# First block of a four-layer kernel: selection ahead of the angles, tokens in another order, sums and weights split, column product on VectorE

## The reference

```
xn   = layernorm(x);   x2 = layernorm(xn) * g_in + b_in
s    = (xn Wq)(ctx Wk)^T per head (4 heads, 77 keys), masked
keep the 32 largest scores of each row; softmax over them; mean of the heads, token mask
film = (attention @ ctx Wv) @ [W_film_in, W_film_out] + biases, times a gate
xk   = x2 * (1 + film_in_gain) + film_in_shift
K[d, l] = 2 Re sum_n dC[d, n] exp(dtA[d, n] l),  l = 0..511      (S4D kernel)
y    = causal convolution of xk with K (by a transform of length 1024) + xk * D_skip
xt   = y * (1 + film_out_gain) + film_out_shift + xn
x    = x + layernorm(xt + gelu(layernorm(xt) W1 + b1) W2 + b2) * g_out + b_out
```

## Time and profile before

| | us |
|---|---|
| median of 3 runs (lowest, highest) | 630.66 (626.01, 631.53) |
| the profiled execution | 629.79 |
| its span | 628.0 |
| PE busy in the span | 499.5 |
| DVE busy | 376.9 |
| ACT busy | 269.4 |
| POOL busy | 157.4 |

### The profile page before, as it was taken

How to read it: one execution, slowest core, us unless ns; L and a number is a source line. 1 busy time by engine, 2 the same in 40 slices (tenths; PEclk the granted TensorE clock), 3 DMA queues, 4 the chain that set the end, 5 groups by cost and what they waited for, 6 DMA issues and landing times.

```text
span 628.0 us, 9151 instructions
## 1 busy us (share of the span) xinstructions
PE 499.5 (80%) x3063; PEld 354.9 (57%) x3063; DVE 376.9 (60%) x1354; ACT 269.4 (43%) x830; POOL 157.4 (25%) x187
## 2 busy tenths in 40 slices
PE   4383689879893589995767774998999999879977
PEld 2132679868661256774545543675566666548845
DVE  5499973134537556763466744775444444589866
ACT  3688433340131366652243442662222222199643
POOL 5999952003215500001300452110000000110032
PEclk9557766979896699997565677897999999999999
DMA  8200000000318000000000103000000000000001
GB/s 312 110 1 1 3 2 2 0 1 1 134 32 353 1 1 2 1 3 1 1 7 23 32 11 91 0 3 1 1 1 1 1 0 1 1 2 0 2 1 33
DMA packets 9636, 18.36 MB, mean 29 GB/s; under 512 B 947, under 2 KB 8179, under 8 KB 9078
## 3 DMA queue, kind: packets, MB, share of 16 engines
q1 hardware_dynamic: 9590, 17.79, 7.8%
HBM read 16.00 MB, written 1.79 MB: 28 GB/s over the span
## 4 chain that ended last, share of the span: by engine, by line
PE 62%; POOL 15%; DVE 13%; ACT 4%; issue 3%; DMA 1%; ACTq 0%; SPq 0%; DVEq 0%; POOLq 0%
PE bank L1755 6%; PE bank L1756 6%; PE bank L1766 5%; PE bank L726 3%; PE bank L1010 3%; PE bank L757 3%; PE bank L1941 2%; PE bank L1054 2%; POOL rstd L205 2%; PE bank L1033 2%; DVE stats L196 2%; ACT arenaB L1957 2%; POOL arenaA L608 2%; PE bank L1917 2%; PE bank L1629 2%
## 5 line engine op out<-in xcount | busy, mean ns | idle before, releaser
L204 POOL TENSOR_SCALAR rtmp<-mv 128x4 f32<-128x4 f32 x22 | 5.1, 230 | 333.5 <-DVE mv L190 333.5
L1807 DVE TENSOR_TENSOR arenaB<-arenaB,bank 128x512 f32<-128x512 f32 x40 | 27.5, 688 | 54.7 <-PE bank L1756 53.8
L1777 ACT ACTIVATE arenaB<-bank 128x512 f32<-128x512 f32 x40 | 23.9, 597 | 76.7 <-PE bank L1755 76.7
L1766 PEld LDWEIGHTS bank<-arenaA,arenaB 128*128 128x128 f32 x320 | 38.7, 192 | 9.1 <-issue 9.1
L1755 PE MATMUL bank<-xnT,arenaA 128*128 128x512 f32 x80 | 42.7, 617 | 0.0
L1756 PE MATMUL bank<-xnT,arenaA 128*128 128x512 f32 x80 | 41.7, 604 | 0.0
L1766 PE MATMUL bank<-arenaA,arenaB 128*128 128x128 f32 x320 | 38.8, 275 | 0.0
L1957 ACT ACTIVATE arenaB<-bank,arenaB 128x77 f32<-128x77 f32 x88 | 27.1, 349 | 5.1 <-DVE arenaB L1980 5.1
L240 PE MATMUL bank<-in_ctx,xn 128*128 128x128 f32 x56 | 14.5, 382 | 18.5 <-DVE xn L211 18.4
L1065 DVE TENSOR_REDUCE nmax<-bank 128x1 f32<-128x512 f32 x32 | 20.5, 684 | 11.1 <-PE bank L1010 11.1
L1756 PEld LDWEIGHTS bank<-xnT,arenaA 128*128 128x128 f32 x80 | 15.7, 196 | 20.2 <-issue 20.2
(11 more groups left out here) (475 smaller groups left out, 1296.0 us busy)
## 6 DMA issues: line engine op xcount, KB each, us to landing
arenaA<-in_moe_dram SPq DMA_DIRECT2D x1, 3840.0 KB, 12.4
in_dft<-in_dft_dram SPq DMA_DIRECT2D x1, 2048.0 KB, 10.2
in_dft<-in_head_dram SPq DMA_DIRECT2D x1, 2048.0 KB, 7.6
arenaA<-in_l_dram SPq DMA_DIRECT2D x1, 2048.0 KB, 16.9
vw_scratch<-in_dft SPq DMA_DIRECT2D x32, 38.5 KB
arenaB<-vw_scratch SPq DMA_DIRECT2D x2, 576.0 KB, 4.9
in_rows<-in_rows_dram SPq DMA_DIRECT2D x1, 842.5 KB, 7.3
in_ctx<-in_ctx_dram SPq DMA_DIRECT2D x1, 653.0 KB, 4.3
```

Of the source, the lines that this page charges most:

```text
L1766: ins = nc.tensor.matmul(bank[4 + m % 3][:, q4 * P:(q4 + 1) * P], hid2[:, m % 2, c, q4 * P:(q4 + 1) * P], w[:, 2 * HE + c * P:2 * HE + (c ...
L1777: nc.scalar.activation(sil2[:, n % 3, :], bank[n % 2][:], ACT.Silu).then_inc(silu_ready, 1)
L1807: Vv.tensor_tensor(hid2[:, m % 2, c, :], sil2[:, n % 3, :], bank[2 + n % 2][:], ALU.mult).then_inc(hid_ready, 1)
```

## The change

- **Token order.** Tile q, partition 32g + a now holds token 16a + 4g + q, for x, the masks, the transform tables, `altrow` and `alt` (which gets two columns). In this order `pe_kernel`'s output [32 a, (d, b)] can be copied straight to `kx` by four copies, one for each quarter g. `pe_kernel_turn` and its copies are gone, as is the `unfold` matrix. The input is loaded, and the output stored, by four transfers of 32 partitions each.
- **Loads.** x goes ahead of `ctx`; `dft` is loaded after the phases, because the angles `uG` use its place till then.
- **Selection first.** On ScalarE all score copies go ahead of the angles, the decays between them; the sines come after x2, the first exponents, `vfilm` and `fold1`. On VectorE group 0's four rounds go ahead of `vec_s4`.
- **Column product** from GpSimd to VectorE (`vec_s4_columns`), between group 1's first and second round. `pool_rstd_twice` moves ahead of the `uG` angles, `pool_x2` of batch 0 ahead of the gains.
- **Masks and weights.** `vec_keep0` is split in `vec_mask0` and `vec_weight0`; `vec_film(1)` goes ahead of group 3's rounds.
- **TensorE.** film(1) ahead of kernel(2), the first batch's transform around kernel(3). The Nyquist sums of both batches and the kernel are one call after film(3), and their product one VectorE instruction (`vec_nyquist`).
- **ScalarE.** `act_dft` goes behind film(2) and the sums of group 3.
- **Feed-forward** batch by batch: turn 0, first product 0, turn 1, second product 0, first product 1, second product 1. The hidden values move from arenaA to arenaB. The last layer's weight sums move behind the last film group (ScalarE) and behind the feed-forward (TensorE).

The core of the diff (indentation shortened by eight columns):

```diff
--- before.py
+++ after.py
...
 kny = sb("kny", 1, D)
 yny = sb("yny", 1, NB, D)
 xt = sb("xt", P, NT, D)
-hT0 = part(arenaA, 8192, 4, TOK)
+hT0 = part(arenaB, 0, 4, TOK)
 altrow = arenaA[0:1, 11776:11776 + S]
 consts_set, ctx0_mm, ctx0_copy, bias_rows = sem("consts_set"), sem("ctx0_mm"), sem("ctx0_copy"), sem("bias_rows")
...
-vH, uG = part(arenaB, 4928, D, LH), part(arenaB, 2464, D, LB)
-rH, hh4, eH = part(arenaA, 0, D, LH), part(arenaA, 2176, D, LA), part(arenaA, 6272, D, LA)
+vH, uG = part(arenaA, 0, D, LH), part(packed["dft"], 0, D, LB)
+rH, hh4, eH = part(arenaB, 8416, D, LH), part(arenaA, 2176, D, LA), part(arenaA, 6272, D, LA)
 gg4, sG, eG = (part(arenaB, 8416 + 2048 * i, D, LB) for i in range(3))
-ka = part(arenaA, 6272, D, LB)[0:LA]
-kTl = part(arenaA, 3200, S)
+V_H, V_GC, V_GS, V_HH = 3, 4, 5, 6
 s4_vec, s4_pe, s4_inverses = sem("s4_vec"), sem("s4_pe"), sem("s4_inverses")
+def quarters():
+    return [slice(LA * g, LA * (g + 1)) for g in range(P // LA)]
+def tokens(v, g):
...
 def sync_loads(sp):
-    for k in ("cols", "ctx"):
-        sp.dma_start(packed[k][:], A[k]).then_inc(loaded[k][0], 16)
-    sp.dma_start(X[:], A["x"].rearrange("(t p) d -> p t d", p=P)).then_inc(x_loaded, 16)
+    sp.dma_start(packed["cols"][:], A["cols"]).then_inc(loaded["cols"][0], 16)
+    for g, r in enumerate(quarters()):
+        sp.dma_start(X[r].rearrange("p (b q) d -> p b q d", b=NB), tokens(A["x"], g)).then_inc(x_loaded, 16)
+    sp.dma_start(packed["ctx"][:], A["ctx"]).then_inc(loaded["ctx"][0], 16)
     sp.dma_start(packed["s4"][:], A["s4"]).then_inc(loaded["s4"][0], 16)
     sp.dma_start(masks8[:], A["masks"].partition_broadcast(P)).then_inc(masks_loaded, 16)
     sp.dma_start(tmask8[:], A["tmask"]).then_inc(masks_loaded, 16)
...
     sp.dma_start(altrow, A["altrow"]).then_inc(bias_rows, 16)
-    for k in ("dft", "l3f", "l1", "ffn0", "small0", "l2"):
+    for k in ("l3f", "l1", "ffn0", "small0", "l2"):
         sp.dma_start(packed[k][:], A[k]).then_inc(loaded[k][0], 16)
+    sp.wait_ge(s4_vec, V_GS)
+    sp.dma_start(packed["dft"][:], A["dft"]).then_inc(loaded["dft"][0], 16)
     sp.wait_ge(y_mm, 2 * NB)
     sp.dma_start(packed["head0"], A["head0"]).then_inc(loaded["head0"][0], 16)
...
                 ins = nc.vector.match_replace(r0[:, t, h, :], top0[:, t, h, 8 * k:8 * k + 8], src[:, t, h, :], NEVER)
         st.link(ins)
-def vec_keep0(dve, st, g):
+def vec_mask0(dve, g):
     for t in GROUPS[g]:
         dve.wait_ge(e0_ready, t + 1)
         nc.vector.scalar_tensor_tensor(e0[:, t], r0[:, t], 0.5 * NEVER, e0[:, t], ALU.is_lt, ALU.mult).then_inc(em_ready, 1)
+def vec_weight0(dve, st, g):
     r = slice(2 * g, 2 * g + 2)
     dve.wait_ge(sums_ready, 2 * g + 2)
...
-A_ARE, A_ANG, A_VH, A_UG, A_GAIN, A_HH = 2, 3, 4, 5, 6, 7
+A_ARE, A_ANG, A_VH, A_UG, A_GAIN = 2, 3, 4, 5, 6
...
     dve.wait_ge(s4_pool, A_VH)
-    vec_phase(st, rH, vH, V["quarter"]).then_inc(s4_vec, 1)
+    vec_phase(st, vH, rH, vH, V["quarter"]).then_inc(s4_vec, 1)
     dve.wait_ge(s4_pool, A_UG)
-    vec_phase(st, gg4, uG, V["quarter"]).then_inc(s4_vec, 1)
-    ins = vec_phase(st, sG, uG, V["off2"])
+    dve.wait_ge(s4_vec, V_H)
+    vec_phase(st, gg4, gg4, uG, V["quarter"]).then_inc(s4_vec, 1)
+    vec_phase(st, sG, sG, uG, V["off2"]).then_inc(s4_vec, 1)
+    dve.wait_ge(s4_vec, V_GS)
+def vec_s4_columns(dve):
+    dve.wait_ge(s4_act, E_COLS)
+    for d in range(0, D, D // 8):
+        r = slice(d, d + D // 8)
+        ins = nc.vector.tensor_tensor(hh4[:, r], hh4[:, r], eH[:, r], ALU.mult)
     ins.then_inc(s4_vec, 1)
-    dve.wait_ge(s4_vec, 5)
 em1, half_sin, full_sin, u0, inv_a2, u1, u2, u3 = (q[i][:] for i in (0, 1, 2, 3, 4, 5, 6, 7))
...
+    pool_rstd_twice(pool, st, 0, False)
     for r in (slice(i * n, (i + 1) * n) for i in range(4)):
         ins = tt(uG[:, r], bc(ang[:, r], P, n, LB), V["iotab"].unsqueeze(1).broadcast_to([P, n, LB]), ALU.mult)
     ins.then_inc(s4_pool, 1)
-def pool_s4_columns(pool):
-    pool.wait_ge(s4_act, 4)
-    for d in range(0, D, D // 8):
-        r = slice(d, d + D // 8)
-        ins = nc.gpsimd.tensor_tensor(hh4[:, r], hh4[:, r], eH[:, r], ALU.mult)
-    ins.then_inc(s4_pool, 1)
-def pool_s4_rows(pool, st):
+def pool_s4_rows(pool, st, slices):
...
-def act_s4_decay(act):
-    A_ = nc.scalar.activation
+def act_s4_tanh(act):
     act.wait_ge(s4_pool, A_ARE)
-    A_(q[0][:], are[:], ACT.Tanh, scale=0.5).then_inc(s4_act, 1)
-    for m in range(LA):
-        a = LA // 2 - 1 - m if m < LA // 2 else m
-        ins = A_(eH[:, :, m], are[:], ACT.Exp, scale=float(LB * a))
-    ins.then_inc(s4_act, 1)
+    nc.scalar.activation(q[0][:], are[:], ACT.Tanh, scale=0.5).then_inc(s4_act, 1)
+def act_s4_decay(act, part):
+    for a in part:
+        ins = nc.scalar.activation(eH[:, :, a], are[:], ACT.Exp, scale=float(LB * a))
+    if part[-1] == LA - 1:
+        ins.then_inc(s4_act, 1)
...
-    A_(hh4[:, :, LA // 2:LA], rH[:, :, 0:LA // 2], ACT.Sin, scale=-TURN, bias=V["qturn"])
-    A_(hh4[:, :, 0:LA // 2], rH[:, :, 1:LH], ACT.Sin, scale=V["lowturn"], bias=V["qturn"]).then_inc(s4_act, 1)
+def act_s4_columns(act):
+    A_ = nc.scalar.activation
+    act.wait_ge(s4_vec, V_H)
+    A_(hh4[:, :, LA // 2:LA], vH[:, :, 0:LA // 2], ACT.Sin, scale=-TURN, bias=V["qturn"])
+    A_(hh4[:, :, 0:LA // 2], vH[:, :, LA // 2:0:-1], ACT.Sin, scale=V["lowturn"], bias=V["qturn"]).then_inc(s4_act, 1)
...
-    pe.wait_ge(s4_pool, A_HH + 1 + i)
+    pe.wait_ge(s4_vec, V_HH)
+    pe.wait_ge(s4_pool, A_GAIN + 1 + i)
     if i >= 2:
...
                                hh4[:, d, :], gg4[:, d, :], start=True, stop=True)
     ins.then_inc(kern_pe, 1)
-def pe_kernel_turn(pe):
-    pe.wait_ge(kern_act, 4)
-    for b in range(LB):
-        ins = nc.tensor.matmul(bank[2][:, b * LA:(b + 1) * LA], ka[:, :, b], V["unfold"][0:LA], start=True, stop=True)
-    ins.then_inc(kern_pe, 1)
-    pe.wait_ge(kern_act, 5)
-    for j in range(TB):
-        ins = nc.tensor.transpose(bank[3][:, j * P:(j + 1) * P], kTl[:, j * P:(j + 1) * P], ident)
-    ins.then_inc(kern_pe, 1)
...
 def act_kernel(act, i):
     per = 512 // LB
     act.wait_ge(kern_pe, i + 1)
-    nc.scalar.copy(ka[:, i * per:(i + 1) * per, :], bank[2 + i % 2][0:LA, :].rearrange("p (d b) -> p d b", b=LB)).then_inc(kern_act, 1)
...
+    for g, r in enumerate(quarters()):
+        src = bank[2 + i % 2][0:LA, :].rearrange("p (d b) -> p b d", b=LB)[:, g * TB:(g + 1) * TB, :]
+        ins = nc.scalar.copy(kx[r, :, i * per:(i + 1) * per], src)
+    ins.then_inc(kern_act, 1)
...
-def pe_nyquist(pe, parts, b):
-    pe.wait_ge(film_ready, TB * (b + 1))
-    for at, v in enumerate(parts):
+def pe_nyquist(pe):
+    pe.wait_ge(xk_ready, NT)
+    for at, v in enumerate((xk[:, 0], xk[:, 1], kx)):
         for q4 in range(TB):
-            ins = nc.tensor.matmul(bank[7][0:1, at * D:(at + 1) * D], V["alt"], v[:, q4], start=(q4 == 0), stop=(q4 == TB - 1))
+            ins = nc.tensor.matmul(bank[4][0:1, at * D:(at + 1) * D], V["alt"][:, q4 % 2:q4 % 2 + 1], v[:, q4], start=(q4 == 0), stop=(q4 == TB - 1))
     ins.then_inc(dft_mm, 1)
...
         tt(out[:, :, 0], pr[:, 0, :, 0], pr[:, 1, :, 1], ALU.subtract)
         tt(out[:, :, 1], pr[:, 1, :, 0], pr[:, 0, :, 1], ALU.add).then_inc(prod_ready, 1)
         dve.wait_ge(prod_ready, 3 * b + jj + 1)
-    dve.wait_ge(kf_ready, 2 + b)
-    tt(yny[:, b], yny[:, b], kny[:], ALU.mult).then_inc(prod_ready, 1)
+def vec_nyquist(dve):
+    dve.wait_ge(kf_ready, 2)
...
     n = 0
     for b in range(NB):
+        pe_turn(pe, ln_done, NT * 1, tmp2, [b])
+        if b:
+            pe_ffn0_down(pe, 0)
         pe.wait_ge(ln_T, NB * 1 + b + 1)
         for c in range(4):
             if n >= 4:
                 pe.wait_ge(ff_gelu, n - 3)
-            nc.tensor.matmul(bank[2 + n % 4][:], V["w1"][:, c * P:(c + 1) * P], xnT[:, b * S:(b + 1) * S],
+            nc.tensor.matmul(bank[4 + n % 4][:], V["w1"][:, c * P:(c + 1) * P], xnT[:, b * S:(b + 1) * S],
                              start=True, stop=True).then_inc(ff_mm, 1)
             n += 1
-    for b in range(NB):
-        pe.wait_ge(ff_gelu, 4 * b + 4)
-        for q4 in range(TB):
-            t = b * TB + q4
-            for c in range(4):
-                ins = nc.tensor.matmul(bank[6 + b][:, q4 * P:(q4 + 1) * P], hT0[:, c, t * P:(t + 1) * P],
-                                       V["w2"][:, c * P:(c + 1) * P], start=(c == 0), stop=(c == 3))
-        ins.then_inc(ff_out, 1)
+    pe_ffn0_down(pe, 1)
+def pe_ffn0_down(pe, b):
+    pe.wait_ge(ff_gelu, 4 * b + 4)
+    for q4 in range(TB):
+        t = b * TB + q4
+        for c in range(4):
+            ins = nc.tensor.matmul(bank[2 + b][:, q4 * P:(q4 + 1) * P], hT0[:, c, t * P:(t + 1) * P],
+                                   V["w2"][:, c * P:(c + 1) * P], start=(c == 0), stop=(c == 3))
+    ins.then_inc(ff_out, 1)
...
     sync_fold3(sp)
     sp.wait_ge(x4_added, NT)
-    sp.dma_start(out.rearrange("b (q p) d -> p (b q) d", p=P), X[:]).then_inc(stored, 16)
-    sp.wait_ge(stored, 16)
```

(87 more changed lines are left out.)

69 lines of the change are left out of this document (31 added, 38 removed).

## The result

The changed kernel took 608.50 us (median of 4 runs, 606.55 to 611.81) against 631.10 (626.01 to 631.93): ratio 0.966, 95% interval 0.960 to 0.972. 613.3 was forecast. Its profiled execution took 607.13 us, 22.7 less than the one read before.

What follows compares the result with a forecast made beforehand. The first block's chain was taken as on GpSimd until about 80 us, then TensorE, with VectorE full as well. Gains 14.1 (to B) + 2.8 (after B) - 0.4 (output) = 16.5; 629.8 - 16.5 = 613.3 us, range 603 to 623.

Steps and rivals of the forecast that it cites:

- W: Time at which the first group's weights are ready on VectorE; forecast 62.6 us, 3.4 later than before.
- W to B: Stretch from first weights ready to start of back transform; forecast 69.6 us, bounds 66 and 73, against 87.1 before.
- B: Start of the back transform on TensorE; forecast 132.2 us, 14.1 earlier than the 146.28 before.
- back transform at 129 to 135: Sign that the forecast is right: the back transform starts at 129 to 135 us.
- 481.7 us less about 2.5: Stretch from the back transform's start to the end; the forecast counts as wrong if it isn't this.
- rival 2: TensorE stays at 2.4 GHz because its queue has fewer gaps from film(1) on; 608.5 us, chance 0.13.
- Column product 7.0: Column product on VectorE takes 7.0 us, between 4.9 and the 10.32 it took on GpSimd.
- Rival 1: Port lock: column instructions alternate fully with GpSimd's gains, columns 8.6 to 10.3, W 67; 617.5 us, chance 0.22.
- Rival 3: Column product waits for ScalarE's sines and blocks VectorE's queue; slower from 60.2 on, 636.6 us at 67; chance 0.04.
- The spectrum wait: New TensorE wait before batch 1's transform, until ScalarE copies the kernel's spectrum behind film(2) and group 3's sums; 4.6 us.
- Rival 4: VectorE's queue, not TensorE, sets film(2) and film(3), needing 14 us more on VectorE; 627 us, chance 0.06.
- After B: Feed-forward by batch gains 2.8 us: 0.7 from a start gap, 2.1 at VectorE's residual; output stores cost 0.4.

Runs made afterwards that it cites:

- e3: Changed kernel with ScalarE's spectrum copy (act_dft) moved ahead of film(2) and group 3's sums; 612.96 us.
- e6: Changed kernel with the feed-forward in its old order (both turns, both first products, both second); 613.88 us.
- e7: Changed kernel with the context's load issued ahead of x again; 608.03 us.
- e8: Changed kernel with ScalarE's spectrum copy placed between film(2)'s diagonals and the rest of film(2); 605.46 us.
- c1: The changed kernel run again unedited, as a control; 607.97 us.
- e4: Kernel before, without the turn: four quarter copies straight to kx, old token order, so it convolves with another kernel; 617.84 us.
- e9: Changed kernel with group 0's mask and weights three selection rounds earlier on VectorE, and film(0) ahead of group 1's sums on ScalarE; 604.00 us.
- e5: Changed kernel with the old front: sines ahead of scores, vec_s4 ahead of group 0's selection, x2 behind the gains; 625.89 us.
- e1: Changed kernel with GpSimd's gains waiting until VectorE's column product is done; 607.85 us.
- e2: Changed kernel with the column product back on GpSimd, behind the gains and ahead of the rows; 608.30 us.
- e11: Changed kernel with the moves of e8 and e9 together and the context's load first, as in e7; 596.80 us.

## Why the prediction was right, step by step

The direction, the range (603 to 623) and the mechanism held; 608.5 is 4.8 under the forecast. Part of this is luck, since the parts held less well than the sum: W came 2.7 late, W to B, 63.2, lies under the lower bound that I had set (66), and the gain behind B was twice what I gave it. By the letter two signs came out against me: back transform at 129 to 135 (128.5), and 481.7 us less about 2.5 from there to the end (476.8, so less 4.9). That it is rival 2's very time is half chance: its mechanism came true up to film(2), not for the second batch's transform, and the stretch behind B made up the difference.

- **W = 62.6, measured 65.3.** Start +2.1 (17.7, past my bound of 17; the other profiles with this front have 16.9 to 19.0): I had only ScalarE's copy in mind and moved it 1 us forward for the earlier load of x. The load did come early, but the context now lands later, and VectorE waits for GpSimd's power of it (L514, 1.21 idle). Phases +0.8 (13.3). Masks and weights +0.6: two instructions beside GpSimd's rows. Against these, group 0 and four rounds -0.5, columns -0.3.
- **Column product 7.0, measured 6.7**, between 4.90 alone and 11.92 beside the rows. Rival 1 (8.6 to 10.3) had the right mechanism and the wrong neighbour: gain operations are short. Its W of 67 was closer than mine, its B wasn't.
- **Rival 3** (columns late for ScalarE's sines) didn't occur: no idle time before 46.37. The margin was small, since ScalarE's second sine ended at 45.67, not at 43.
- **W to B 69.6, measured 63.2.** This is the term that was mis-sized. By its own steps: film(0) -1.1, both kernels -0.2, to film(1)'s end -0.9, to the end of the kernel transform -2.1 (first batch's transform at 7.7, not 9.45), film(2) -2.0 (3.6, not 5.6). I had carried durations at the lower level over from the earlier trace rows into a queue that no longer had the gaps that came before them. Not all of it is the edit's: in e3, e6, e7 and e8, whose code on TensorE is the same up to the kernel's transform, film(0)'s start to that transform took 31.8 to 32.1 us, in the changed kernel and c1 29.8 and 29.9. So some 2 of the 6.4 us depend on the execution; the first batch's transform ran at full level (3.84 twice) in all six. Against rival 2, I argued that gaps of 3 to 5 us remain; one of 3.5 does (before 79.42), and the level is back at full before the third kernel at 84.82. e4 shows the same transform at 3.84 twice with only the turn gone.
- **The spectrum wait 4.6, measured 4.4**, and half the transform behind it at the lower level, 6.3 of 6.2. The last piece to B: 10.5 as forecast.
- **Hidden edits.** Transform tables: no wait for them in TensorE's rows. Row slices: early enough; with W 6.5 us earlier and GpSimd untouched (e9) they begin to bind. Rival 4 had VectorE's slack at 13 us; not measured directly, but its part of film(2) releases TensorE in 0.37 once the spectrum wait is gone (e8).
- **After B, -2.8, measured -5.3.** The 2.1 behind the product was right (e6). The start gap that I put at 0.7 is worth 2.5 with the level behind it. VectorE now waits 2.29 for the product: "late next is the product itself" held. Output and rest: +0.4, as forecast, but this stretch differs by up to 5.9 us among the profiles, so the agreement is luck; which part of it is the four stores wasn't taken apart.

It was faster by more than 1%, which had a chance of 0.91. What the sum hid is how the parts hang together: e4 shows that leaving out the turn, which the new token order allows, gives 12.5 us at B by itself, and e5 that with the old front the new kernel's B is back at the old one's.

## What to carry to other kernels

When an edit closes gaps in TensorE's queue, as this one did, take the durations of what follows from rows at full level and make the lower level the rival, not the other way round: here that was 4 to 6 of the 22.7 us. Before a call that waits is moved forward on an engine that takes its calls in order, list what was issued ahead of it and used the waiting time (e3, 0.6 us gained), and split the call so that this part stays (e8, 5.2). A stage's worth is read from where its edit begins to where it ends: e3's loss at B lay ahead of its edit. Work moved between two engines that both feed the same consumer moves only a milestone (e1, e2); reordering within the queue that is late, without touching the other, moved the time (e9).

## What the runs showed of the hardware

- VectorE's tensor_tensor with both inputs in SBUF and GpSimd's tensor_tensor alternate instruction by instruction, so the price of running side by side is set by the length of the neighbour's instructions: the same eight instructions took 4.90, 6.73 and 11.92 us.
- TensorE's level differs between profiled executions for the same instructions in the same place: from film(0)'s start to the first kernel 4.94 us (the changed kernel), 4.97 (c1), 6.23 (e6, e7), 6.38 (e8), 6.43 (e3). With film(1) it moves the kernel's transform by some 2 us, more than small edits do. The kernel profiled twice agrees with itself, and the four slower ones have edits elsewhere in the program, though those of e3, e6 and e8 come later in every engine's order; whether it is chance or the edits isn't settled.
- The unedited rest after the residual took 439.4 to 440.1 us in seven profiled executions (the kernel before and the changed one among them) and 441.7 to 445.3 in the other seven. The longest, e3, shows a granted clock of 0.94 from 412 to 605 us, the second row below; the changed kernel had 0.98 there, the first row. Over the whole span, e3's four runs (611.0 to 614.8 us) had mean clocks of 0.840 to 0.849, c1's 0.856 to 0.859; but a run of the changed kernel itself, 611.8 us, had 0.841. Whether e3's edit shifted the clock so far behind it isn't shown. e8 to e11, which shared a chip, all show about 442. The kernel before took the same time on that chip as on the other two (630.8 against 630.6 and 630.7), which speaks against the chip; where these 2 us come from stays open.

```profile
412.00:605.00 193.00, 176.96 (x899) 118.72 (x899) 116.82 (x319) 79.86 (x272) 15.11 (x25) 0.98 0.01 4
```

```profile
412.00:605.00 193.00, 181.14 (x886) 121.29 (x885) 114.11 (x311) 79.16 (x269) 15.08 (x25) 0.94 0.00 1
```
